# Convolution taps and softplus read PSUM, a product moves to GpSimd, norms and head masks to ScalarE

## The chip, the cores and the metric

The kernel runs on one core of a Trainium2 chip. The metric is the device time of one execution in microseconds. Names of engines in the rows: PE is TensorE, DVE VectorE, ACT ScalarE, POOL GpSimd, SP SyncE.

## The reference, cut to what matters

Sixteen sequences of 512 tokens by 256 features, all fp32, go through two blocks with residuals. "Block 0" is a quadratic-kernel attention with 16 heads of 16 features and an int8-weight gated FFN; "block 1" is a two-way Mamba and an FFN whose operands are quantised to FP4.

```python
x = x + attn(layernorm(x)); x = x + ffn_int8(layernorm(x))
x = x + bimamba(layernorm(x)); x = x + ffn_fp4(layernorm(x))
# attn, per head: A = (q k^T)**2 * causal; o = A v / (A.sum(-1) + eps)
# bimamba(x): xn = norm(x) * g + b; x + mamba(xn, f) + flip(mamba(flip(xn), b))
# mamba: u = silu(causal_conv4(u) + convb)             512 channels
#        dt = softplus(dtr @ Wdt.T + bdt); A = -exp(Alog)
#        h_t = exp(dt_t * A) * h_{t-1} + (dt_t * u_t) * B_t    16 states
#        y_t = sum_n h_t[n] * C_t[n];  y = (y + u * D) * silu(z) @ Wout.T
# q(x) = fp4(x / s) * s per block of 16, s = max|x| / 6
```

## The kernel before

**Timetable.** The recurrence sets the frame. One sequence has 2 directions x 16 states x 4 channel tiles = 128 *slots*; in slot j VectorE runs one `tensor_tensor_scan` over 512 tokens (`scan`, L1216). Around it, with fixed offsets in slots, GpSimd makes the input product B x (dt u) three slots ahead (`inflow`, L714), ScalarE the decay exp(dt A) into PSUM two slots ahead (`decay`, L923), TensorE turns a state back to tokens with four transposes four slots later (`turn_state`, L1501, two PSUM banks HT[0] and HT[1]), VectorE adds half of the turned states weighted by C (`add_state`, L1227), and ScalarE with GpSimd the other half (`weigh_last` L931, `add_last` L725). A state (4 slots) has three buffers, the decay three PSUM banks. So the engines can be a few slots apart and no more.

**The rest of the model** is laid beside this by hand: `PLAN` says for each engine and slot which pieces it issues after the slot's own work (`row(piece, direction, ahead, PE=[...], ACT=[...], ...)`, L285 to L371; `side` issues them). Each engine issues in this order, so a piece that waits holds everything behind it on its engine, the next scan too. While the Mamba of sequence b runs, the attention and int8 FFN of b+1, the FP4 FFN of b-1 and the first steps of b+2 run in its gaps. Direction r=1 is the first half of the slots, its convolution at slots 14 to 25 and its softplus at 35 to 46; r=0 of the next sequence has them at 91 to 98 and 105 to 111.

**PSUM.** Three banks (`SB`) serve all side pieces. `bank_of` gives each product the bank longest unused in the order of `PLAN`; `take_bank` (L411) makes TensorE wait until the reader of the bank's last user is done (`LEAVES` names the signal). From slot 14 to 51 the bank `SUMS` belongs to the attention's weighted sums, so that two are left (`HELD`).

**The pieces that the change touches.** `norm` (L1029) for the five layer norms: three small operations for 1/sqrt, then four `tensor_scalar` of 128x256 (L1042). `attn_q`: a projection of q for 8 heads (L1295) is multiplied by four 0/scale columns to isolate heads, two on ScalarE (L780), two on VectorE (L1062); the four results lie in `qm`, read by the scores (`score`, L1310) of 24 score steps; the second half's projection at PE slot 28 follows the last score of the first. `project` (L844): ScalarE copies the product into the padded `upad` (L856) and writes tap 3 with the bias (L857); `convolve` (L1156): VectorE adds the other three taps from `upad`. `softplus` (L873): Abs and Relu from PSUM (L879, L880), Exp (L882) and Ln (L886) in SBUF; `softplus_rest` (L1169, L1171) makes a rounding correction, `softplus_sum` (L697, L700) adds both on GpSimd, `step_size` (L1176) forms dt u on VectorE. `attn_divide` (L1068) waits for the turned sums.

## Time and profile before

| | |
|---|---|
| time, median of 3 runs | 6962.02 us (6948.84 to 6964.09) |
| the profiled execution: time, span | 6966.85 us, 6965.1 us |
| mean granted TensorE clock | 0.803 |
| one sequence, from a scan to the same scan of the next | 416.2 us |

The page gives busy times of engines over the span; each instruction group by line with what ended the idle time before it; the chain of waits that ended last. Since the sequences repeat, a table of busy times over the stretches of one sequence shows what each part of the timetable is bound by. The sequence that starts at 3231.79 us is used: slot 8 is at 3249.54, 24 at 3293.27, 40 at 3352.37, 48 at 3377.62, 64 at 3423.56, 80 at 3472.24, 96 at 3524.82, 112 at 3591.08 and its end at 3647.94.

### The profile page before, as it was taken

The numbers are of one execution on the slowest core, as the hardware profiler recorded it, in microseconds if no ns is written. First come the engines' busy times: TensorE is split into PE (matmuls) and PEld (weight loads), VectorE is DVE, ScalarE is ACT, GpSimd is POOL, SyncE is SP. The second block draws the span as 40 slices with busy tenths as digits, with TensorE's granted clock in tenths as the row PEclk, the third lists the DMA queues.
The fourth block names the chain that finished last, engine by engine and source line by source line (L and its number), as shares of the span: only waits on it lengthen the run. The fifth ranks groups of instructions, "written<-read, shape, count | busy, mean of one in ns | idle before, by whom it ended". The sixth has DMA issues, their size and how long they took to land.

```text
span 6965.1 us, 83507 instructions
## 1 busy us (share of the span) xinstructions
PE 5063.0 (73%) x21853; PEld 3220.5 (46%) x21900; DVE 5281.2 (76%) x6580; ACT 4022.4 (58%) x6424; POOL 4972.3 (71%) x3786
## 2 busy tenths in 40 slices
PE   3776777868777686877868777676877768777665
PEld 2344444544444444544444444444544444444444
DVE  3277788787878778788787878878787787878884
ACT  1365665656656565655656656565665656656563
POOL 0177877777777777777778777777777777777894
PEclk6688888878878788887878878788887878888777
DMA  3011111111111111111111111111111111111110
GB/s 107 25 36 40 43 48 49 34 50 43 39 50 50 44 34 44 45 48 50 45 43 39 38 51 48 45 33 44 47 48 48 47 43 38 40 48 45 37 46 25
DMA packets 152821, 309.07 MB, mean 44 GB/s; under 512 B 20870, under 2 KB 58310, under 8 KB 149926
## 3 DMA queue, kind: packets, MB, share of 16 engines
q1 hardware_dynamic: 152278, 302.80, 13.5%
q8 instruction: 222, 3.64, 0.2%
q14 instruction: 321, 2.63, 0.1%
HBM read 285.90 MB, written 16.84 MB: 43 GB/s over the span
## 4 chain that ended last, share of the span: by engine, by line
PE 32%; issue 21%; DVE 17%; POOL 17%; ACT 10%; DMA 0%; DVEq 0%; POOLq 0%; SPq 0%; ACTq 0%
POOL arena_m L714 7%; PE psum L1310 7%; PE psum L1501 6%; DVE arena_m L1216 5%; POOL arena_m L725 5%; PE psum L1354 3%; DVE arena_m L1227 2%; PE psum L1273 2%; PE psum L1443 2%; PE psum L1481 2%; ACT hc L931 2%; ACT L759 2%; PE psum L1417 2%; PE psum L1389 1%; DVE arena_m L1156 1%
## 5 line engine op out<-in xcount | busy, mean ns | idle before, releaser
L714 POOL TENSOR_TENSOR arena_m<-bS,arena_m 128x512 f32<-128x512 f32 x2048 | 2703.6, 1334 | 394.7 <-PE psum L1501 358.7
L1216 DVE TENSOR_TENSOR_SCAN arena_m<-psum,arena_m 128x512 f32<-128x512 f32 x2048 | 2452.0, 1209 | 138.4 <-POOL arena_m L714 58.0
L923 ACT ACTIVATE psum<-arena_m,Aneg 128x512 f32<-128x512 f32 x2048 | 1414.8, 694 | 1387.1 <-DVE arena_m L1216 1355.7
L1501 PE MATMUL psum<-ident,arena_m 128*128 128x128 f32 x8192 | 1491.2, 317 | 858.2 <-DVE arena_m L1227 643.5
L725 POOL TENSOR_TENSOR arena_m<-arena_m,hc 128x512 f32<-128x512 f32 x1024 | 1362.9, 1331 | 821.1 <-ACT hc L931 766.5
L1501 PEld LDWEIGHTS psum<-ident,arena_m 128*128 128x128 f32 x8192 | 1121.2, 162 | 1563.4 <-issue 601.3
L1227 DVE SCALAR_TENSOR_TENSOR arena_m<-psum,Ct,arena_m 128x512 f32<-128x512 f32 x1024 | 746.4, 729 | 286.2 <-PE psum L1501 261.3
L1310 PE MATMUL psum<-arena_a 64*128 64x512 f32 (+3 forms) x2048 | 789.0, 517 | 98.7 <-ACT arena_a L790 49.3
L931 ACT ACTIVATE hc<-psum,Ct 128x512 f32<-128x512 f32 x1024 | 695.0, 679 | 229.4 <-PE psum L1501 172.8
L790 ACT ACTIVATE arena_a<-psum 128x384 f32<-128x384 f32 (+1 forms) x768 | 399.6, 526 | 356.1 <-PE psum L1310 352.4
L1310 PEld LDWEIGHTS psum<-arena_a 64*128 64x128 f32 x2048 | 382.9, 214 | 353.4 <-issue 217.1
L1156 DVE SCALAR_TENSOR_TENSOR arena_m<-arena_m,convw 128x512 f32<-128x512 f32 x384 | 421.3, 1098 | 103.4 <-ACT arena_m L857 98.5
L1389 PE MATMUL psum<-wB,arena_a 128*128 128x352 f32 x1024 | 426.4, 549 | 6.3 <-ACT arena_m L880 4.8
L671 POOL TENSOR_TENSOR arena_a<-arena_a 128x704 f32<-128x704 f32 (+1 forms) x80 | 152.3, 1904 | 375.8 <-DVE arena_a L982 375.8
L1354 PE MATMUL psum<-arena_a,wA 128*128 128x512 bf16 x1105 | 323.8, 441 | 104.5 <-ACT arena_m L896 55.9
L662 POOL TENSOR_SCALAR_AFFINE_SELECT arena_a<-arena_a 128x512 f32<-128x512 f32 (+1 forms) x192 | 186.3, 970 | 259.4 <-ACT arena_a L790 259.3
L1408 PE MATMUL psum<-ident,arena_a 128*128 128x128 f32 (+1 forms) x384 | 89.3, 398 | 311.6 <-POOL arena_a L677 311.6
L1176 DVE TENSOR_TENSOR arena_m<-arena_m 128x512 f32<-128x512 f32 x128 | 218.7, 1709 | 110.9 <-POOL arena_m L700 110.9
L1265 PE MATMUL psum<-ident,arena_a 128*128 128x128 f32 x640 | 131.6, 373 | 226.3 <-DVE arena_a L1042 201.4
L1426 PE MATMUL psum<-xnT,wU 128*128 128x512 f32 x512 | 264.0, 642 | 4.7 <-ACT arena_m L857 2.0
L1434 PE MATMUL psum<-xnT,wZ 128*128 128x512 f32 x512 | 264.9, 644 | 0.0
L1389 PEld LDWEIGHTS psum<-wB,arena_a 128*128 128x128 f32 x1024 | 213.8, 231 | 90.4 <-issue 41.8
(151 smaller groups left out, 7524.0 us busy)
## 6 DMA issues: line engine op xcount, KB each, us to landing
bS<-brow SPq DMA_DIRECT2D x512, 256.0 KB, 3.2
wB<-kept_B SPq DMA_DIRECT2D x16, 1408.0 KB, 6.8
wU<-kept_U SPq DMA_DIRECT2D x32, 512.0 KB, 4.3
wZ<-kept_Z SPq DMA_DIRECT2D x32, 512.0 KB, 4.5
wO<-kept_O SPq DMA_DIRECT2D x32, 512.0 KB, 4.8
wA<-kept_A SPq DMA_DIRECT2D x16, 768.0 KB, 7.0
...
```

Of the source, the lines that this page charges most:

```text
L714: pool.tensor_tensor(hb[s % HBS][:, m, :], bS[:, s % 2, :], du[r][:, m, :], ALU.mult).then_inc(m_dbu.sem, 1)
L725: pool.tensor_tensor(yT[:, 2 + i, :], yT[:, 2 + i, :], hc[:, i, :], ALU.add).then_inc(m_yl.sem, 1)
L790: act.activation(asq[:, gu % 2, j, 0:n], bank("a_score", None, w)[:, 0:n], ACT.Square).then_inc(a_sq.sem, 1)
L923: act.activation(EB[j % EBS], dt[r][:, m, :], ACT.Exp, scale=Aneg[:, r, m, n:n + 1]).then_inc(m_dA.sem, 1)
L931: act.activation(hc[:, i, :], HT[1], ACT.Copy, scale=Ct[:, r, 2 + i, n:n + 1]).then_inc(m_hc.sem, 1)
L1156: dve.scalar_tensor_tensor(u[:, m, :], upad[:, m % 2, tap:tap + T], convw[:, r, m, tap:tap + 1], u[:, m, :], ALU.mult, ALU.add).then_inc(m ...
L1216: dve.tensor_tensor_scan(v, EB[j % EBS], v, 0.0, ALU.mult, ALU.add).then_inc(m_scan.sem, 1)
L1227: dve.scalar_tensor_tensor(yT[:, i, :], HT[0], Ct[:, r, i, n:n + 1], yT[:, i, :], ALU.mult, ALU.add).then_inc(m_y.sem, 1)
L1310: ins = pe.matmul(bank("a_score", None, w)[:, c:c + n], kT[rows, ht, i * P:(i + 1) * P], qm[rows, j, i * P:T], start=True, stop=True)
L1354: ins = pe.matmul(bank(piece, None, m), w[:, k, m * P:(m + 1) * P], xparts[:, c, k, :], start=(k == 0 and c == 0), stop=(k == KD - 1 and c ...
L1389: ins = pe.matmul(bank(piece, None, w)[:, 0:FIH], xTq[:, k, i * P:(i + 1) * P], w_[:, k, c * FIH:(c + 1) * FIH], start=(k == 0), stop=(k = ...
L1501: ins = pe.transpose(HT[pos % 2][:, m * P:(m + 1) * P], hb[s % HBS][:, m, i * P:(i + 1) * P], ident[:, :])
```

## The change

1. **Convolution.** `upad`, its copy and its zero pads go. ScalarE writes tap 3 to `u`; the three others are read by VectorE from PSUM, shifted by writing to `u[late:]`, all three in one slot. The bank is free only when the third tap is done.
2. **Softplus.** `ex` goes: Abs and Exp stay in the PSUM bank, and the correction reads it there, now after Ln. The bank is free at the end of the correction instead of after Relu.
3. **dt u** moves to GpSimd, right behind the two additions of the same tile.
4. **Norms.** VectorE keeps the small operations, one more of them (`shift` = -mean x rstd); ScalarE does the 128x256 ones, a slot later.
5. **Head masks** are all on ScalarE. The second half's q is projected right behind the first's (slots 125 and 126 of the sequence before) and copied to `qraw`; each of its masks is written as soon as the last score that reads that slice of `qm` is done.
6. **Timetable.** Consumers come later: the chain from `a_onturn` to the Mamba's `m_turn` moves by 1 to 7 slots, r=0's convolution from 91 to 99, its softplus from 105 to 112. `z_in` of r=1 moves from 80 to 77. The FP4 FFN starts 2 slots earlier (`q_gate` at 88, not 90), and its turn comes 10 slots behind a token tile's first product, not 9. r=1's ScalarE and VectorE steps come one slot earlier. `xTq` has its own place, and a bank that is open between two pieces is not given out.

```diff
-            row("p_conv", r, ahead, DVE=[j0 + c + k for c in late for k in (2, 2, 3)])
+            row("p_conv", r, ahead, DVE=[j0 + c + 2 - r for c in late for k in range(PAD)])
...
-            "p_in": (1, lambda r, n: [(m_up, 2 * (NM * r + n + 1))]), "p_x": (2, lambda r, n: [(m_xd, r + 1)]),
-            "p_c": (1, lambda r, n: [(m_ct, r + 1)]), "p_dt": (1, lambda r, n: [(m_rl, NM * r + n + 1)]),
+            "p_in": (1, lambda r, n: [(m_conv, PAD * (NM * r + n + 1))]), "p_x": (2, lambda r, n: [(m_xd, r + 1)]),
+            "p_c": (1, lambda r, n: [(m_ct, r + 1)]), "p_dt": (1, lambda r, n: [(m_c2, NM * r + n + 1)]),
...
+                pool.wait_ge(*m_sum.by(b, 2 * q + 2))
+                pool.tensor_tensor(du[r][:, m, :], dt[r][:, m, :], u[:, m, :], ALU.mult).then_inc(m_du.sem, 1)
...
+            def norm(b, n, src, dst):
+                act.wait_ge(*ln_scale[n].by(b, 4))
+                for i in range(NT):
+                    act.activation(dst[:, i, :], src[:, i, :], ACT.Identity, scale=rstd[:, n, i:i + 1],
+                                   bias=shift[:, n, i:i + 1]).then_inc(ln_out[n].sem, 1)
...
             def attn_q(b, _, h):
                 act.wait_ge(*a_q_ps.by(b, h + 1))
-                for j in range(2):
+                if h:
+                    act.copy(qraw[:, :], bank("a_q", None, h)).then_inc(a_qr.sem, 1)
+                    return
+                for j in range(G):
                     act.activation(qm[:, j, :], bank("a_q", None, h), ACT.Copy, scale=qmask[:, j:j + 1]).then_inc(a_qa.sem, 1)
+            def attn_qmask(b, _, j):
+                act.wait_ge(*a_s_ps.by(b, NG * NU * G // 2 - G + j + 1))
+                act.wait_ge(*a_qr.by(b, 1))
+                act.activation(qm[:, j, :], qraw[:, :], ACT.Copy, scale=qmask[:, j:j + 1]).then_inc(a_qa.sem, 1)
...
-                act.copy(upad[:, m % 2, PAD:PAD + T], src).then_inc(m_up.sem, 1)
...
-                act.activation(ex[:, c, :], src, ACT.Abs, bias=bdt[:, r, m:m + 1]).then_inc(m_ab.sem, 1)
                 act.activation(dt[r][:, m, :], src, ACT.Relu, bias=bdt[:, r, m:m + 1]).then_inc(m_rl.sem, 1)
+                act.activation(src, src, ACT.Abs, bias=bdt[:, r, m:m + 1]).then_inc(m_ab.sem, 1)
                 act.wait_ge(*m_ab.by(b, q + 1))
-                act.activation(ex[:, c, :], ex[:, c, :], ACT.Exp, scale=-1.0).then_inc(m_ex.sem, 1)
+                act.activation(src, src, ACT.Exp, scale=-1.0).then_inc(m_ex.sem, 1)
...
-                dve.scalar_tensor_tensor(u[:, m, :], upad[:, m % 2, tap:tap + T], convw[:, r, m, tap:tap + 1], u[:, m, :],
+                dve.scalar_tensor_tensor(u[:, m, late:T], src[:, 0:T - late], convw[:, r, m, tap:tap + 1], u[:, m, late:T],
                                          ALU.mult, ALU.add).then_inc(m_conv.sem, 1)
...
-                dve.wait_ge(*m_ex.by(b, q + 1))
+                dve.wait_ge(*m_ln.by(b, q + 1))
```

Three places of the instruction order follow, each before and then after. In them lines of the change are numbered anew: L939, L947 are the decay and `weigh_last`, L811 the squared score, L801 the mask from `qraw`, L1210 the scan, L1221 `add_state`, L719 `inflow`, L730 `add_last`, L674 to L680 the tail of the FP4 rounding (L671 to L677 before).

ScalarE where the attention's second half of heads begins, slots 26 to 29, before:

```order
L790 ACTIVATE arena_a<-psum 128x384
L923 ACTIVATE psum<-arena_m,Aneg 128x512
L790 ACTIVATE arena_a<-psum 128x384 x2
L923 ACTIVATE psum<-arena_m,Aneg 128x512
L931 ACTIVATE hc<-psum,Ct 128x512
L790 ACTIVATE arena_a<-psum 128x384
L923 ACTIVATE psum<-arena_m,Aneg 128x512
L780 ACTIVATE arena_a<-psum,qmask 128x512 x2
L790 ACTIVATE arena_a<-psum 128x512
```

The same place of the change:

```order
L811 ACTIVATE arena_a<-psum 128x384
L939 ACTIVATE psum<-arena_m,Aneg 128x512
L801 ACTIVATE arena_a<-qraw,qmask 128x512 x2
L811 ACTIVATE arena_a<-psum 128x384 x2
L939 ACTIVATE psum<-arena_m,Aneg 128x512
L947 ACTIVATE hc<-psum,Ct 128x512
L801 ACTIVATE arena_a<-qraw,qmask 128x512 x2
L811 ACTIVATE arena_a<-psum 128x384
L939 ACTIVATE psum<-arena_m,Aneg 128x512
L811 ACTIVATE arena_a<-psum 128x512
```

Two masks behind the last score of the first half have become four, two of them ahead of the last three squared scores, and none needs a product of TensorE in between.

VectorE at the first convolution of r=1, slots 13 to 16, before (L1216 and L1210 are the scan):

```order
L1227 SCALAR_TENSOR_TENSOR arena_m<-psum,Ct,arena_m 128x512
L1216 SCALAR_TENSOR_TENSOR arena_m<-psum,arena_m 128x512 x2
L1227 SCALAR_TENSOR_TENSOR arena_m<-psum,Ct,arena_m 128x512
L1156 SCALAR_TENSOR_TENSOR arena_m<-arena_m,convw 128x512 x2
L1216 SCALAR_TENSOR_TENSOR arena_m<-psum,arena_m 128x512
L1156 SCALAR_TENSOR_TENSOR arena_m<-arena_m,convw 128x512
```

The same place of the change:

```order
L1221 SCALAR_TENSOR_TENSOR arena_m<-psum,Ct,arena_m 128x512
L1210 SCALAR_TENSOR_TENSOR arena_m<-psum,arena_m 128x512
L1160 SCALAR_TENSOR_TENSOR arena_m<-psum,convw,arena_m 128x509
L1160 SCALAR_TENSOR_TENSOR arena_m<-psum,convw,arena_m 128x510
L1160 SCALAR_TENSOR_TENSOR arena_m<-psum,convw,arena_m 128x511
L1210 SCALAR_TENSOR_TENSOR arena_m<-psum,arena_m 128x512
```

The taps of a tile stand together, a slot earlier, and read PSUM.

GpSimd at the softplus of r=0, the second of its four tiles, slot 108 before:

```order
L714 TENSOR_TENSOR arena_m<-bS,arena_m 128x512
L697 TENSOR_TENSOR arena_m<-arena_m 128x512
L700 TENSOR_TENSOR arena_m<-arena_m 128x512
L714 TENSOR_TENSOR arena_m<-bS,arena_m 128x512
L725 TENSOR_TENSOR arena_m<-arena_m,hc 128x512
L671 TENSOR_TENSOR arena_a<-arena_a 128x704
```

The same tile in the change, slot 115 (the first tile's three operations stand behind L674, in slot 114):

```order
L674 TENSOR_TENSOR arena_a<-arena_a 128x704
L700 TENSOR_TENSOR arena_m<-arena_m 128x512
L703 TENSOR_TENSOR arena_m<-arena_m 128x512
L705 TENSOR_TENSOR arena_m<-arena_m 128x512
L719 TENSOR_TENSOR arena_m<-bS,arena_m 128x512
L730 TENSOR_TENSOR arena_m<-arena_m,hc 128x512
L677 TENSOR_TENSOR arena_a<-arena_a 128x704
L680 TENSOR_TENSOR arena_a<-arena_a 128x704
L700 TENSOR_TENSOR arena_m<-arena_m 128x512
L703 TENSOR_TENSOR arena_m<-arena_m 128x512
L705 TENSOR_TENSOR arena_m<-arena_m 128x512
L719 TENSOR_TENSOR arena_m<-bS,arena_m 128x512
```

L705 is dt u. The four tiles now fall in four slots in a row, 114 to 117, together with the last FP4 rounding.

## Rows read from the trace of the kernel before

**Rows 1.** The page: span, and part 1, busy time of each engine.
```profile
span 6965.1 us, 83507 instructions
...
PE 5063.0 (73%) x21853; PEld 3220.5 (46%) x21900; DVE 5281.2 (76%) x6580; ACT 4022.4 (58%) x6424; POOL 4972.3 (71%) x3786
```

**Rows 2.** Part 4 of the page: the chain that ended last, by engine.
```profile
PE 32%; issue 21%; DVE 17%; POOL 17%; ACT 10%; DMA 0%; DVEq 0%; POOLq 0%; SPq 0%; ACTq 0%
```

**Rows 3.** Busy time by stretch, one sequence: stretch, length, engines, PEclk, DMA share, GB/s.
```profile
3249.54:3293.27 43.73, 43.52 (x201) 26.06 (x200) 37.54 (x46) 29.65 (x53) 40.51 (x32) 0.96 0.16 50
3293.27:3352.37 59.10, 52.62 (x204) 26.67 (x202) 35.62 (x40) 37.95 (x66) 35.98 (x31) 0.80 0.07 23
3352.37:3377.62 25.25, 23.14 (x107) 11.89 (x107) 20.85 (x23) 19.14 (x35) 25.02 (x20) 0.86 0.07 23
3377.62:3423.56 45.94, 25.29 (x123) 17.78 (x123) 38.38 (x56) 23.84 (x36) 34.04 (x27) 0.74 0.17 58
3423.56:3472.24 48.68, 42.36 (x230) 31.61 (x231) 37.24 (x46) 29.60 (x41) 36.38 (x28) 0.93 0.10 32
3472.24:3524.82 52.58, 40.09 (x156) 24.65 (x154) 44.53 (x71) 34.37 (x53) 36.43 (x27) 0.87 0.21 73
3524.82:3591.08 66.26, 41.62 (x159) 26.92 (x160) 54.32 (x62) 46.21 (x70) 51.18 (x36) 0.79 0.04 13
3591.08:3647.94 56.86, 31.36 (x134) 22.75 (x133) 43.86 (x56) 20.69 (x36) 39.01 (x31) 0.71 0.23 71
```

**Rows 4.** The same view, 20 us inside the second stretch.
```profile
3309.00:3329.00 20.00, 18.68 (x44) 7.84 (x44) 7.51 (x8) 8.26 (x15) 11.14 (x10) 0.61 0.00 1
```

**Rows 5.** Groups by shape, VectorE: what is removed or changed; busy us, mean ns, idle.
```profile
L1156 DVE SCALAR_TENSOR_TENSOR arena_m<-arena_m,convw 128x512 f32<-128x512 f32 x384 | 421.3, 1098 | 103.4 <-ACT arena_m L857 98.5
...
L1171 DVE TENSOR_TENSOR arena_m<-arena_m 128x512 f32<-128x512 f32 x128 | 178.0, 1390 | 4.4
...
L1176 DVE TENSOR_TENSOR arena_m<-arena_m 128x512 f32<-128x512 f32 x128 | 218.7, 1709 | 110.9 <-POOL arena_m L700 110.9
...
L1169 DVE TENSOR_SCALAR arena_m<-arena_m 128x512 f32<-128x512 f32 x128 | 86.8, 678 | 3.6 <-ACT arena_m L882 3.6
...
L1042 DVE TENSOR_SCALAR arena_a<-xA,mv,ve 128x256 f32<-128x256 f32 x192 | 118.1, 676 | 1.2
...
L1042 DVE TENSOR_SCALAR arena_a<-arena_a,mv,ve 128x256 f32<-128x256 f32 x64 | 43.7, 742 | 0.6
...
L1042 DVE TENSOR_SCALAR arena_a<-xF,mv,ve 128x256 f32<-128x256 f32 x64 | 22.9, 421 | 0.0
...
L1062 DVE TENSOR_SCALAR arena_a<-psum,qmask 128x512 f32<-128x512 f32 x64 | 45.1, 746 | 108.8 <-ACT arena_a L780 108.8
```

**Rows 6.** Timeline around 3530 and 3589 us: start us, us, engine, line, operation.
```profile
3527.30 0.75 DVE L1156 SCALAR_TENSOR_TENSOR arena_m<-arena_m,convw 128x512 f32<-128x512 f32 x1
...
3530.18 2.82 DVE L1156 SCALAR_TENSOR_TENSOR arena_m<-arena_m,convw 128x512 f32<-128x512 f32 x2
...
3530.34 2.11 POOL L671 TENSOR_TENSOR arena_a<-arena_a 128x704 f32<-128x704 f32 x1 [7.29 <-DVE arena_a L982]
...
3589.35 1.26 POOL L714 TENSOR_TENSOR arena_m<-bS,arena_m 128x512 f32<-128x512 f32 x1
```

**Rows 7.** Groups by shape: the nearest rows to what is added.
```profile
L1227 DVE SCALAR_TENSOR_TENSOR arena_m<-psum,Ct,arena_m 128x512 f32<-128x512 f32 x1024 | 746.4, 729 | 286.2 <-PE psum L1501 261.3 <-ACT arena_m L896 24.7
...
L714 POOL TENSOR_TENSOR arena_m<-bS,arena_m 128x512 f32<-128x512 f32 x2048 | 2703.6, 1334 | 394.7 <-PE psum L1501 358.7 <-DMA bS<-brow 33.9
...
L857 ACT ACTIVATE arena_m<-psum,convb,convw 128x512 f32<-128x512 f32 x128 | 101.0, 789 | 0.0
...
L827 ACT COPY arena_a<-psum 128x352 f32<-128x352 f32 x128 | 57.7, 450 | 31.5 <-PE psum L1389 31.4
...
L1034 DVE SCALAR_TENSOR_TENSOR lnv<-mv 128x4 f32<-128x4 f32 x80 | 50.2, 628 | 3.1 <-ACT mv L767 3.1
```

**Rows 8.** Groups by shape: the wait for the turned sums.
```profile
L1068 DVE RECIPROCAL rz<-psum 128x16 f32<-128x16 f32 x64 | 16.3, 255 | 178.3 <-PE psum L1333 178.3
```

More of the change, by code:

```diff
@@ L324, in block_kernel @@
[L324 to L338 removed]
+            row("q_up", None, -1, first=2 * i, PE=[j + 3, j + 4], DVE=[j + 4, j + 6])
@@ new lines, in block_kernel @@
+            row("q_hquant", None, -1, first=QHEAD * i, DVE=[j + 6, j + 6, j + 6, j + 7, j + 7, j + 8])
+            row("q_htail", None, -1, first=QTAIL * i, POOL=[j + 8, j + 9, j + 9])
+            row("q_hturn", None, -1, first=2 * i, PE=[j + 10, j + 10], ACT=[j + 11, j + 11])
+            row("q_down", None, -1, first=i, PE=[j + 12], DVE=[j + 13])
+        for j, r, ahead in ((30, 1, 0), (107, 0, 1)):
+            row("p_x", r, ahead, PE=[j, j + 1], ACT=[j + 2])
+            row("p_rows", r, ahead, SP=[j + 3])
+            row("p_c", r, ahead, PE=[j + 4], DVE=[j + 5])
@@ L390, in block_kernel @@
         }
[L391 removed]
+        HELD = range(14, 53)
         jobs_of = [[], [], []]
```

227 lines of the change are left out of this document (99 added, 128 removed).

## The prediction

> **What bounds the kernel now.** I start with the page. Over the span VectorE is busy 76%, TensorE 73%, GpSimd 71% [rows 1]: no engine is full. The chain that ended last is spread over all of them, with TensorE 32%, VectorE and GpSimd 17% each, ScalarE 10% and 21% in which nothing is seen to run [rows 2]. So the kernel is bound by different engines in turn and by the hand-overs between them, and VectorE's sum alone decides nothing. The next view is one sequence cut into stretches [rows 3]; slots 0 to 8, the 17.8 us ahead of its first row, are not touched. The reader should compare each stretch with its busiest engine. Slots 8 to 24 (first row) take 43.7 us and TensorE is busy 43.5: full. Slots 24 to 40 take 59.1 with TensorE at 52.6, at a granted clock of 0.80. Slots 40 to 48 are GpSimd's (25.0 of 25.3). Slots 48 to 64 take 45.9, VectorE 38.4. Slots 64 to 80 lie nearest to TensorE (42.4 of 48.7), slots 80 to 96 to VectorE (44.5 of 52.6). Slots 96 to 128 take 123.1, VectorE 98.2 and GpSimd 90.2, and the end holds some us of the loop's own turn.
>
> **VectorE's sum.** Removed: the 128x256 norms, 118.1 + 43.7 + 22.9 = 184.7 us, the masks, 45.1, and dt u, 218.7 [rows 5]. The 384 taps take 1098 ns now [rows 5]; the same operation with one operand in PSUM takes 729 [rows 7], so they save 384 x 0.369 = 142. The 128 subtractions at 1390 ns [rows 5] become the like, 128 x 0.66 = 85 saved. The addition beside them goes from 678 to about 729, +7, and the 80 `shift` operations cost some 628 ns each, +50 [rows 7]. Together 618 us, 39 per sequence.
>
> Why a tap costs 1098 is seen in the timeline: one alone takes 0.75 us, two beside a GpSimd addition take 1.41 each, and GpSimd's L671 takes 2.11 [rows 6]. The two engines hold each other up when VectorE reads two operands from SBUF. GpSimd's product takes 1.26 alone [rows 6] against a mean of 1.334 [rows 7], so GpSimd would get back up to 2048 x 0.07 = 150 us if all such meetings ended.
>
> The Trainium skill (VectorE: DVE Perf Modes, "Why PSUM operands drop a tier") speaks against the other half of the softplus edit: one-source fp32 operations run twice as fast only between SBUF tensors. The trace shows L1169 between SBUF tensors at a mean of 678, no better than a PSUM operation here; if its mean were half of 729, the edit would lose 128 x 0.36 = 47 us of VectorE instead of 7.
>
> **ScalarE.** Added are 320 norms of 256 columns. Their price lies between a plain copy of 352 columns, 450 ns, and a scaled and biased one of 512, 789 ns [rows 7]; for 256 columns I take 570, nearer the lower end: 182 us. The 80 more masks and q copies stand against the 128 copies to `upad` that go, about zero. ScalarE comes to 4200 us, 60%. That is hidden where ScalarE waits; between slots 26 and 29 it gets four masks for two, which the waits that go there cover.
>
> **GpSimd.** 128 x 1.27 = 163 us more, 10 per sequence: that is a term on the path where GpSimd is full.
>
> **Where the time comes and goes, per sequence.**
> - Slots 8 to 24: **+4**. A convolution's bank was free after two ScalarE operations; now it waits for ScalarE's 0.8 and three taps of 0.73, about 3.3 us with the hand-overs. TensorE has 1.5 to 2.4 us of other work before it needs that bank for the second score of the next slot. It stalls at slots 17, 20 and 23, 0.9 to 1.8 us each, 4.4 together, less some for the shorter VectorE part; behind it wait the transposes of the state. Bounds: -1 (the taps are done in time) and +8 (each waits a scan more).
> - Slots 24 to 40: **-7**. The masks of the second half no longer stand in a row after a new projection. TensorE ran at half its clock from 3309 to 3329 us: 18.7 us busy at a granted 0.61, for the most part at the lower of its two levels, 1.2 of 2.4 GHz [rows 4]; at full clock that is 18.7 x 0.61 = 11.4, or 7.3 less, and its idle 1.3 us goes. VectorE's wait for the turned sums, 178 us in all or 11 per sequence, two of its four places here [rows 8], ends in part, since its piece now comes a slot later. Against it: ScalarE's softplus of 4 operations and the correction now hold a bank about 4.7 us at slots 35 and 38, with 2.5 us of cover, so +4.4 if nothing hides it; I count half. Bounds: -12 and +2.
> - Slots 40 to 48: **+4**. Three dt u on the full engine, 3 x 1.27. The two bank stalls there, 2.2 us each, lie beside GpSimd's work. Bounds +3 and +5.
> - Slots 48 to 64: **-7**. Eight norm operations leave VectorE (8 x 0.58 = 4.6), and the projection behind the attention gets a slot more between its steps, so that VectorE does not stand before it. Bounds: -10 and -2.
> - Slots 64 to 80: **+2**. The int8 FFN starts 5 slots later with the same TensorE work, after a longer idle time in which the clock falls (0.74 in the stretch ahead, [rows 3]). Bounds -1 and +4.
> - Slots 80 to 96: **-6**. Eight norm operations, 4 x 0.676 + 4 x 0.742 = 5.7 us, and eight taps of r=0, 8.8, leave VectorE [rows 5]; FP4 and int8 pieces that move in and four small operations fill part of it, and ScalarE's norms now stand between the steps of a chain. I count less than half. Bounds: -9 and -1.
> - Slots 96 to 128: **-4**. VectorE loses four dt u, 6.8, four norms, 2.7, four longer subtractions, 2.6, two masks, 1.5, and has twelve taps at 0.73 for four at 1.10, +4.4: 9.2 less. GpSimd gets the four softplus tiles in slots 114 to 117: 4 x 3 x 1.27 = 15.2, three FP4 operations of at most 2.1 each [rows 6], 6, and its own 4 x (1.27 + 0.64) = 7.6, in all 29 us for four slots; the product for the scan three slots on stands behind them, and VectorE has fewer pieces than that in these slots. What VectorE wins before that is largely waited for here. Bounds: -14 and +6.
>
> Sum: 4 - 7 + 4 - 7 + 2 - 6 - 4 = **-14 us per sequence**, 224 for sixteen (the first and last are partly alone, which I leave out). The profiled execution took 6966.85 us, 5 more than the median of the runs. 6966.85 - 224 = 6743; against the median 6738. I predict **6740 us**.
>
> **Rivals.**
> 1. *Held banks decide, slower.* The place is TensorE behind p_in and p_dt with two banks. If VectorE is a scan and an addition late at the third tap, each of the first three stalls is 3 us instead of 1.4, and slots 8 to 24, 43.5 us of TensorE at 0.96, run at the 0.80 of the next stretch: 43.5 x 0.96/0.80 - 43.5 = 8.7. With that and no clock won back in slots 24 to 40 (-1 for -7) the sum is 3 x 3 + 8.7 - 1, and -11 for the other five terms: +6, or 7060 us. For: TensorE is full there. Against: VectorE has fewer and shorter operations just there, and ScalarE's step comes a slot earlier. The sign turns when the seven stalls are 2 us longer each than I assume. The Trainium skill (TensorE: Matmul & The Clock Gate, Part 1) says that throttled is the default and activity releases it; that would make this rival costlier than its stalls. Chance 0.13.
> 2. *All of VectorE's time comes back.* If every stretch gave VectorE's 39 us, 16 x 39 = 618, the time would be 6350. For: VectorE is the busiest engine, and GpSimd gains too. Against: TensorE and GpSimd would then need 311 us each within 378, closer than in any long stretch now but the first. The Trainium skill (SBUF — State Buffer, "Who interferes with whom") says that only VectorE operations with two SBUF inputs or in a 2-port mode meet GpSimd, so that with one operand in PSUM both gain. Between 6500 and this: chance 0.12.
> 3. *Nothing but waiting moves.* The load leaves VectorE, but each stretch is set by hand-overs (21% of the chain, [rows 2]) and the gains of slots 24 to 40 fail, -1 for -7, and 48 to 64, -2 for -7: so 3 us less per sequence in place of 14: 6920, with the places nearest to no change among its outcomes. Chance 0.08.
> 4. *GpSimd's cluster costs the gain at the end*, +6 for -4, so 4 us less per sequence in all: 6900. For: the count above. Against: GpSimd's bound stretch before, 104 to 111, held eight such additions too. Chance 0.05.
>
> **How the numbers follow.** The forecast case, 6540 to 6860, has 0.62. The distances of the bounds from the seven terms, taken together as independent, give about 16 us per sequence upward and 13 downward: 6990 and 6530. I stretch the lower end to 6480 for the nearer part of the second rival; the range is **6480 to 6990**. Within 0.2% is about what a measurement of this kernel can tell from no change. Faster by more: 0.62 + 0.12 + most of rivals 3 and 4 = 0.83. The same: 0.04, from rival 3. Slower: 0.13.
>
> **What would show it.** In the profile after: taps at 0.70 to 0.75 us with or without GpSimd beside them; VectorE's busy time near 4660 us; norms on ScalarE near 0.57; TensorE waiting for VectorE's third tap in score products at slots 17, 20, 23, 1 to 2 us each; slots 24 to 40 shorter with a clock above 0.9; GpSimd full at slots 114 to 118 with scans waiting for its product. I am wrong if TensorE's waits behind held banks pass 3 us each, if slots 24 to 40 keep their 59 us, or if 96 to 128 grow.

## The result and the profile after

The changed kernel takes **6918.5 us** (median of 11 runs, 6890.6 to 6958.3) against 6962.0 (11 runs); the ratio is 0.9942, 95% interval 0.9921 to 0.9962. It is faster by 0.6%, not by the 3.2% of the forecast: the direction is right, the time lies in the range, the size is missed by 179 us. The kernel before took 6962 us beside the change and 6948 to 6953 beside the experiments below, so differences across them are good to about 10 us. One run of e4 (9407 us) and one of e12 (13041 us) lie far above the others of their kernel and enter no ratio.

The page of the kernel after, span and part 1 [rows 1], and part 4, the chain [rows 2]:

```profile
span 6935.8 us, 82733 instructions
...
PE 5245.0 (76%) x21900; PEld 3287.9 (47%) x21900; DVE 4746.4 (68%) x6116; ACT 4128.6 (60%) x6696; POOL 4905.2 (71%) x3914
...
PE 41%; issue 19%; POOL 18%; DVE 10%; ACT 9%; DMA 2%; POOLq 0%; SPq 0%; DVEq 0%; ACTq 0%
```

VectorE lost 535 us of work, and the span 29. TensorE has the same matmuls and is busy 182 us longer (some 20 of them because 47 matmuls are missing from the trace before); its share of the chain rose from 32 to 41%. The mean granted clock is 0.803, as before. So the load went away, and the end is now set more by TensorE and what it stands for.

The groups by shape, kernel after (busy us, mean ns | idle before and what ended it) [rows 5, 7, 8]:

```profile
L719 POOL TENSOR_TENSOR arena_m<-bS,arena_m 128x512 f32<-128x512 f32 x2048 | 2599.3, 1285 | 183.2 <-PE psum L1493 155.3 <-DMA bS<-brow 26.1 <-issue 1.2
...
L778 ACT ACTIVATE arena_a<-xA,shift,ve 128x256 f32<-128x256 f32 x192 | 99.7, 594 | 61.4 <-DVE shift L1055 61.4
...
L872 ACT ACTIVATE arena_m<-psum,convb,convw 128x512 f32<-128x512 f32 x128 | 99.2, 775 | 204.4 <-PE psum L1418 204.1
...
L1160 DVE SCALAR_TENSOR_TENSOR arena_m<-psum,convw,arena_m 128x509 f32<-128x509 f32 x128 | 95.2, 744 | 190.6 <-ACT arena_m L872 190.6
...
L1176 DVE TENSOR_TENSOR arena_m<-psum,arena_m 128x512 f32<-128x512 f32 x128 | 88.5, 691 | 4.4
...
L1174 DVE TENSOR_SCALAR arena_m<-psum 128x512 f32<-128x512 f32 x128 | 87.9, 687 | 309.9 <-ACT arena_m L899 268.0 <-POOL arena_m L703 41.9
```

The durations are those of the prediction: taps 744 to 750 ns for 729, norms 594 for 570, the subtraction 691. The idle column is not. The first tap (L1160) stood 191 us for ScalarE's tap 3 (98.5 in [rows 5]) and the correction (L1174) 268 us for ScalarE's Ln, where its predecessor L1169 waited 3.6 [rows 5]. ScalarE itself stood 204 us for the projection.

The waits of the whole span, kernel after (us in total, times, longest). L1303 is the squared score's product, L1176 and L1160 VectorE's last readings of a softplus's and a convolution's bank, L892 the softplus's first operation and L899 its Ln, L872 ScalarE's tap 3:

```profile
DVE arena_m L1174 <- ACT arena_m L899: 268.0, 67, 8.0
...
ACT arena_m L892 <- PE psum L1448: 213.4, 97, 4.0
...
ACT arena_m L872 <- PE psum L1418: 204.1, 87, 5.4
...
DVE arena_m L1160 <- ACT arena_m L872: 190.6, 78, 9.4
...
PE psum L1303 <- DVE arena_m L1176: 127.1, 60, 2.9
...
PE psum L1381 <- DVE arena_m L1160: 81.3, 28, 3.6
...
PE psum L1303 <- DVE arena_m L1160: 70.1, 45, 2.0
...
PE psum L1448 <- DVE arena_m L1176: 44.8, 16, 3.2
```

The two of L1303 are the held banks that the prediction named: 105 stalls, 2.1 and 1.6 us each. The other two stalls of TensorE behind VectorE it did not count: the FP4 FFN's products (L1381) stand behind the convolution of r=0, and the softplus's own products (L1448) behind the correction, 126 us together. The four waits of VectorE and ScalarE were not in it either. They are one chain: TensorE's product and ScalarE's reading are in one slot, VectorE's reading is in the next, and each engine stands until the one ahead of it is done, with the next scan behind it.

The relief of VectorE did reach TensorE: its transposes of the state waited 643.5 us for VectorE's `add_state` before and wait 285.3 us after. The span is shorter by 29 us all the same.

Busy time by stretch of the sequence that starts at 3207.27 us (columns as in [rows 3]; slots 8 to 24, 24 to 40, 40 to 48, 48 to 64, then 80 to 96):

```profile
3227.48:3278.88 51.40, 46.03 (x195) 26.82 (x194) 35.71 (x49) 28.27 (x50) 37.05 (x32) 0.90 0.14 44
3278.88:3338.09 59.21, 52.67 (x190) 26.38 (x190) 31.57 (x38) 36.30 (x62) 35.84 (x31) 0.73 0.07 21
3338.09:3370.00 31.91, 27.11 (x95) 14.42 (x95) 15.34 (x20) 18.99 (x35) 22.84 (x20) 0.66 0.08 17
3370.00:3410.96 40.96, 26.84 (x139) 18.09 (x138) 31.11 (x42) 26.94 (x43) 37.02 (x31) 0.79 0.18 61
...
3461.25:3508.84 47.59, 38.43 (x168) 27.81 (x167) 38.17 (x60) 34.86 (x56) 34.09 (x27) 0.82 0.25 81
```

Slots 8 to 24 took 43.73 us and take 51.40, at a clock of 0.90 for 0.96; slots 40 to 48 took 25.25 and take 31.91, at 0.66 for 0.86, and GpSimd, full there before, idles 9 us. From slot 48 on the gains are there.

Single sequences differ by some us, so the same cut is averaged over ten sequences (the fourth to the thirteenth), from the starts of the scans in the trace, in us; e-numbers are the experiments below.

```
slots      0-8   8-24  24-40  40-48  48-64  64-80  80-96  96-128   sum
before    17.8   43.8   59.1   25.2   46.0   48.7   52.6   123.2  416.4
after     19.6   52.6   56.8   31.2   40.6   49.5   47.3   114.7  412.2
e1        18.8   51.5   50.4   32.8   41.6   48.3   46.6   115.1  405.1
e2        19.6   52.4   53.9   25.1   40.7   49.1   47.1   115.3  403.2
e3        19.3   52.1   49.3   23.6   41.6   49.3   46.6   114.2  395.9
e4        19.8   56.1   69.5   41.8   41.5   48.7   47.4   114.4  439.2
e5        19.2   50.3   63.3   32.5   41.5   49.4   47.3   114.9  418.4
e6        17.8   51.4   49.4   26.8   39.0   49.0   46.4   113.8  393.6
e7        20.2   52.3   49.3   23.6   45.3   48.8   52.4   114.3  406.2
e8        17.8   51.4   52.1   27.8   41.1   49.8   47.8   117.5  405.1
e9        17.4   47.1   56.6   29.2   40.2   49.5   47.3   118.1  405.4
e10       19.1   44.3   52.1   25.2   36.2   49.3   47.1   116.2  389.5
e11       17.7   51.5   69.9   33.1   48.2   48.7   52.6   120.9  442.7
e12       17.7   50.4   70.8   32.2   50.3   48.9   52.6   123.1  446.1
```

Ten sequences win 4.2 us each, 42 in all; the first scan starts 21 us earlier; the other six sequences and the end give 34 back, 22 of them in the fifteenth, which took 391 us before and 413 after (why is not shown). Together that is the 29 us between the spans.

Slots 24 to 40 are not alike in the ten sequences of the changed kernel. The shortest and the longest:

```profile
4109.42:4159.31 49.89, 43.17 (x194) 22.51 (x194) 31.25 (x38) 36.73 (x63) 35.81 (x31) 0.90 0.08 25
...
4924.11:4983.33 59.22, 52.67 (x190) 26.36 (x190) 31.58 (x39) 36.30 (x62) 35.83 (x31) 0.73 0.07 22
```

TensorE's busy time times its clock is nearly the same, 38.9 and 38.4 us, and so is its idle time, 6.7 and 6.6 us: the work is equal, and the 9 us between the two are the granted clock. Two of the ten have the short form (49.9 and 51.2 us, at 0.90 and 0.85), eight take 57.6 to 59.2 us at 0.73 to 0.79; the sequence shown above is one of the longest. On average the clock there is 0.79, for 0.78 before, and in e3 it is 0.90 in all ten. What tips a sequence one way or the other was not found.

### The profile page after: what moved, and what is told of

The parts are those of the page before. It is cut to its first block, busy times and chain, and to the rows that moved or that the text cites. A ratio compares the mean times of both kernels' runs of the same rounds, so it can differ in the third digit from the quotient of the medians.

```text
span 6935.8 us, 82733 instructions
## 1 busy us (share of the span) xinstructions
PE 5245.0 (76%) x21900; PEld 3287.9 (47%) x21900; DVE 4746.4 (68%) x6116; ACT 4128.6 (60%) x6696; POOL 4905.2 (71%) x3914
## 4 chain that ended last, share of the span: by engine, by line
PE 41%; issue 19%; POOL 18%; DVE 10%; ACT 9%; DMA 2%; POOLq 0%; SPq 0%; DVEq 0%; ACTq 0%
PE psum L1303 9%; POOL arena_m L719 9%; PE psum L1493 8%; POOL arena_m L730 5%; PE psum L1347 3%; PE psum L1473 3%; PE psum L1426 3%; PE psum L1363 2%; DVE arena_m L1160 2%; PE psum L1418 2%; PE psum L1318 2%; DVE arena_m L1210 2%; POOL arena_a L677 2%; PE psum L1448 1%; PE psum L1435 1%
## 5 line engine op out<-in xcount | busy, mean ns | idle before, releaser
L719 POOL TENSOR_TENSOR arena_m<-bS,arena_m 128x512 f32<-128x512 f32 x2048 | 2599.3, 1285 | 183.2 <-PE psum L1493 155.3
L1210 DVE TENSOR_TENSOR_SCAN arena_m<-psum,arena_m 128x512 f32<-128x512 f32 x2048 | 2448.4, 1210 | 345.4 <-ACT psum L939 170.2
L1493 PE MATMUL psum<-ident,arena_m 128*128 128x128 f32 x8192 | 1524.6, 323 | 661.3 <-DVE arena_m L1221 285.3
L730 POOL TENSOR_TENSOR arena_m<-arena_m,hc 128x512 f32<-128x512 f32 x1024 | 1307.3, 1277 | 1009.6 <-ACT hc L947 829.4
L1493 PEld LDWEIGHTS psum<-ident,arena_m 128*128 128x128 f32 x8192 | 1166.0, 167 | 1413.7 <-issue 738.4
L939 ACT ACTIVATE psum<-arena_m,Aneg 128x512 f32<-128x512 f32 x2048 | 1397.6, 689 | 389.9 <-DVE arena_m L1210 375.3
L1221 DVE SCALAR_TENSOR_TENSOR arena_m<-psum,Ct,arena_m 128x512 f32<-128x512 f32 x1024 | 750.5, 733 | 512.4 <-PE psum L1493 511.0
L1303 PE MATMUL psum<-arena_a 64*128 64x512 f32 (+3 forms) x2048 | 895.3, 568 | 227.9 <-DVE arena_m L1176 127.1
L947 ACT ACTIVATE hc<-psum,Ct 128x512 f32<-128x512 f32 x1024 | 693.9, 678 | 362.9 <-PE psum L1493 278.7
L811 ACT ACTIVATE arena_a<-psum 128x384 f32<-128x384 f32 (+1 forms) x768 | 400.8, 524 | 547.2 <-PE psum L1303 546.6
L1303 PEld LDWEIGHTS psum<-arena_a 64*128 64x128 f32 x2048 | 411.8, 230 | 589.7 <-issue 288.1
L1381 PE MATMUL psum<-wB,arena_m 128*128 128x352 f32 x1024 | 451.0, 575 | 97.3 <-DVE arena_m L1160 81.3
L1160 DVE SCALAR_TENSOR_TENSOR arena_m<-psum,convw,arena_m 128x509 f32<-128x509 f32 (+2 forms) x384 | 286.9, 747 | 199.6 <-ACT arena_m L872 190.6
L674 POOL TENSOR_TENSOR arena_a<-arena_a 128x704 f32<-128x704 f32 (+1 forms) x80 | 144.6, 1807 | 366.9 <-DVE arena_a L998 366.9
L1347 PE MATMUL psum<-arena_a,wA 128*128 128x512 bf16 x1152 | 307.8, 411 | 102.1 <-ACT arena_m L909 38.9
L1381 PEld LDWEIGHTS psum<-wB,arena_m 128*128 128x128 f32 x1024 | 218.7, 236 | 202.3 <-DVE arena_m L1160 74.6
L1174 DVE TENSOR_SCALAR arena_m<-psum 128x512 f32<-128x512 f32 x128 | 87.9, 687 | 309.9 <-ACT arena_m L899 268.0
L1426 PE MATMUL psum<-xnT,wZ 128*128 128x512 f32 x512 | 255.1, 623 | 1.5 <-DVE xM L1193 1.5
L1473 PE MATMUL psum<-wO,arena_m 128*128 128x256 f32 x1024 | 245.8, 384 | 0.9 <-DVE arena_m L1184 0.9
```

The lines of the kernel that those rows point to most:

```text
L719: pool.tensor_tensor(hb[s % HBS][:, m, :], bS[:, s % 2, :], du[r][:, m, :], ALU.mult).then_inc(m_dbu.sem, 1)
L730: pool.tensor_tensor(yT[:, 2 + i, :], yT[:, 2 + i, :], hc[:, i, :], ALU.add).then_inc(m_yl.sem, 1)
L939: act.activation(EB[j % EBS], dt[r][:, m, :], ACT.Exp, scale=Aneg[:, r, m, n:n + 1]).then_inc(m_dA.sem, 1)
L947: act.activation(hc[:, i, :], HT[1], ACT.Copy, scale=Ct[:, r, 2 + i, n:n + 1]).then_inc(m_hc.sem, 1)
L1210: dve.tensor_tensor_scan(v, EB[j % EBS], v, 0.0, ALU.mult, ALU.add).then_inc(m_scan.sem, 1)
L1221: dve.scalar_tensor_tensor(yT[:, i, :], HT[0], Ct[:, r, i, n:n + 1], yT[:, i, :], ALU.mult, ALU.add).then_inc(m_y.sem, 1)
```

## The experiments

**e1, e2, e3: banks given back early.** r=1 alone goes back to copies in SBUF (there is room for one direction only): in e1 its taps read a padded copy, in e2 Abs and Exp of its softplus go to `qraw` and the correction reads it there, after Exp; e3 is both. ScalarE then frees the bank by itself, at the same slots as in the change. r=0 still reads PSUM. (In the diff, `...` stands for lines left out, here and below.)

```diff
-"p_in": (1, lambda r, n: [(m_conv, PAD * (NM * r + n + 1))])
+"p_in": (1, lambda r, n: [(m_up, NM + n + 1), (m_cp, n + 1)] if r else [(m_conv, PAD * (n + 1))])
...
-"p_dt": (1, lambda r, n: [(m_c2, NM * r + n + 1)])
+"p_dt": (1, lambda r, n: [(m_rl, NM + n + 1), (m_ab, NM + n + 1)] if r else [(m_c2, n + 1)])
...
+act.copy(upad[:, m % 2, PAD:PAD + T], src).then_inc(m_cp.sem, 1)
...
+e = qraw[:, :] if r else src
```

> The changed kernel, but direction r=1 (slots 13 to 25, where two banks are left) takes its taps from a padded SBUF copy again; the bank is free after ScalarE's two operations. Held banks decide: the bank waits behind p_in in slots 17, 20, 23 go (45 waits, 70 us in all, behind the taps in the score products) and VectorE no longer gates them; slots 8 to 24 go from 52.8 us back to about 45, the kernel to about 6800 us. Rival, VectorE's early pieces decide (its taps stand a slot earlier and wait for ScalarE, so the scan behind waits): the taps still stand in the same slots, slots 8 to 24 stay above 50 us, 6900 us or more.

> The changed kernel, but the softplus of r=1 keeps Abs and Exp in SBUF (the q copy's place, free then), and frees its bank after Relu and Abs. Held banks decide: TensorE's 60 waits for the correction in the score products, 127 us in all, go; slots 32 to 48 lose about 8 us per sequence, the kernel comes to about 6800 us. Rival, the order of ScalarE's four operations and VectorE's place decide: VectorE still waits for ScalarE's Exp, which ends 0.7 us earlier only, and it meets GpSimd again; less than 3 us per sequence, 6880 us or more.

> Both of the above. Held banks decide: the first half of the slots comes back to what the kernel before needs there or less, 14 to 16 us per sequence, 6680 to 6700 us. Early VectorE pieces decide: 6860 us or more. If both matter the two single runs add up to less than this one.

Measured: e1 6810.2 us (ratio 0.9799, 0.9775 to 0.9823), e2 6766.1 (0.9731, 0.9705 to 0.9757), e3 6664.0 (0.9625, 0.9563 to 0.9687). Against the changed kernel that is 108, 152 and 254 us less. The two are nearly additive, and in this order of the rows the reading of PSUM by VectorE costs 254 us for r=1, though its taps and subtractions got shorter by it. The times are near those expected of held banks. But slots 8 to 24 stay at 51.5 to 52.4: the held bank is not what made them long, as I had expected of e1. The time came back from slot 24 on; in e1 slots 24 to 40 lose 6.4 us, and the granted clock there is 0.86 for 0.79. What is left in slots 8 to 24 is seen in the waits of e3 in that stretch, 3084.51 to 3136.66 us (L884 copies the projection, L885 writes tap 3, L1182 is a tap):

```profile
ACT arena_m L884 <- PE psum L1449: 10.3, 4, 3.6
DVE arena_m L1182 <- ACT arena_m L885: 10.2, 4, 3.7
```

Four tiles, 2.5 us each, on two engines one behind the other. In the same stretch of the kernel before they are 1.3 and 0.2 us, in the changed kernel 10.0 and 11.0.

**e4, e5: r=1's consumers a slot later.** The change puts ScalarE's and VectorE's pieces of r=1 one slot earlier than before (`- r`). e4 takes that back in the changed kernel, e5 in e3. (In e5, and in e10 below, ScalarE also waits for its own Ln of the tile before, since `qraw` is written again.)

```diff
-ACT=[j0 + c + 1 - r for c in late] ... DVE=[j0 + c + 2 - r for c in late for k in range(PAD)]
+ACT=[j0 + c + 1 for c in late] ... DVE=[j0 + c + 2 for c in late for k in range(PAD)]
```

> The changed kernel with r=1's ScalarE and VectorE steps of convolution and softplus one slot later, as in r=0; PSUM still read. Held banks decide: the bank is held longer, TensorE waits more, 6950 to 7050 us. Early VectorE pieces decide: VectorE's waits for Ln (268 us) and for tap 3 (191 us) shrink, the scans are earlier, 6850 us or less.

> The run with both r=1 edits in SBUF, and r=1's ScalarE and VectorE steps a slot later, as in the kernel before. Without held banks a later reader costs TensorE nothing. Theory that the early place blocks the scans (VectorE's 11 us of waits for tap 3 in slots 8 to 24 of one sequence, none before): slots 8 to 24 go from 52.1 to about 44 us, the kernel to about 6540 us. Rival, that these slots are full of TensorE's work at a lower clock and the place is indifferent: 6640 to 6690 us.

Measured: e4 7328.7 us (1.0550, 1.0522 to 1.0579), e5 6995.1 (1.0059, 1.0039 to 1.0079). Every theory failed here. For held banks e4 is too slow by 280 us; for the early place both have the wrong sign, and e5 has no bank held by VectorE. The waits of e5 say who holds it instead (whole span; L1335 is the score's product, L912 and L885 ScalarE's last readings of the two banks, L816 ScalarE's square of the scores):

```profile
ACT arena_a L816 <- PE psum L1335: 859.6, 436, 5.9
...
PE psum L1335 <- ACT qraw L912: 120.6, 60, 2.5
...
PE psum L1335 <- ACT arena_m L885: 91.1, 45, 2.4
```

TensorE waits for ScalarE and ScalarE for TensorE. The kernel before has the same pieces at the same slots and only 352 us of the first wait. What differs is the order within a slot: `side` issues the pieces of a slot in the order of the table's rows, and the change also moved the rows of `p_in`, `p_conv`, `p_silu`, `p_dt` and `p_du` behind the attention's. I had overlooked that in the diff.

**e6, e7, e8: single edits taken back, each in e3.** dt u on VectorE again (e6); the 128x256 norms on VectorE again, their ScalarE slot now VectorE's (e7); the masks again as before, two on each engine, the second projection at slot 28 (e8).

```diff
-pool.tensor_tensor(du[r][:, m, :], dt[r][:, m, :], u[:, m, :], ALU.mult).then_inc(m_du.sem, 1)
+dve.tensor_tensor(du[r][:, m, :], dt[r][:, m, :], u[:, m, :], ALU.mult).then_inc(m_du.sem, 1)
...
-row("f_norm", None, 1, DVE=[61], ACT=[62])
+row("f_norm", None, 1, DVE=[61, 62])
...
-row("a_q", None, 2, PE=[125, 126], ACT=[126, 127])
-row("a_qmask", None, 1, ACT=[27, 27, 28, 28])
+row("a_q", None, 2, PE=[125], ACT=[126], DVE=[126])
+row("a_q", None, 1, first=1, PE=[28], ACT=[29], DVE=[29])
```

> The run with both r=1 edits in SBUF (6664 us), with dt u on VectorE again, two slots later than the additions, as before. If moving it gained what left VectorE (8 products of 1.7 us, 14 us per sequence): 6850 us. If GpSimd is the bound where it went (1.27 us each, slots 40 to 48 and 112 to 118): 6640 us or less. I expect between, 6720 us: a cost of 3 to 4 us per sequence, from the meetings of the two engines more than from the sum.

> The run with both r=1 edits in SBUF, with the twenty 128x256 norm operations of a sequence on VectorE again, in the slot in which ScalarE does them. Theory that VectorE bounds slots 48 to 64 and 80 to 96 (12 operations there, 0.6 us each): 5 to 8 us per sequence more, 6770 us. Rival, that the slots given between the steps did it and the engine is indifferent: 6650 to 6690 us.

> The run with both r=1 edits in SBUF, with the second half's q projected at slot 28 again and its masks split over ScalarE and VectorE. The prediction's term: slots 24 to 40 go from 49.3 us up by 6 to 8 and TensorE's clock falls there, 6770 us. Rival, that the banks did it: within 1 us per sequence, 6680 us.

Measured: e6 6642.8 us (0.9554, 0.9535 to 0.9573), e7 6823.1 (0.9804, 0.9773 to 0.9834), e8 6816.0 (0.9797, 0.9775 to 0.9819). So on e3 the norms on ScalarE are worth 159 us, more than the 106 that I said; the time is in slots 48 to 64 and 80 to 96, 3.7 and 5.8 us per sequence, where the prediction has it. The masks are worth 152, again more than the 106 that I said, but slots 24 to 40 have only 2.8 us per sequence of them, not the 6 to 8 that I had expected; 4.2 are in slots 40 to 48 and 5.0 from slot 64 on. I had expected dt u back on VectorE to cost 56 us. It costs nothing: e6 is the faster by 21 us, which is not clear of noise, since the intervals overlap.

**e9, e10: a slot later, and the rows back ahead of the attention's.** e9 is e4 with the block of rows moved; e10 is e6 with both edits. (With the early place the block can't stand ahead: at slot 34 ScalarE would wait for a product that waits for a score's bank, whose reading stands behind on ScalarE. I read that in the plan; this form was not run.)

```diff
+        for j0, j, r, ahead in ((13, 30, 1, 0), (97, 107, 0, 1)):
+            ...
         row("z_in", 0, 0, PE=[46, 47, 48, 50], ACT=[47, 48, 49, 51])
...
-        for j0, j, r, ahead in ((13, 30, 1, 0), (97, 107, 0, 1)):
-            ...
```

> The changed kernel with r=1's ScalarE and VectorE pieces one slot after the product (as the kernel before has them) and, unlike e4, with the rows of p_in, p_conv, p_dt and p_du back ahead of the attention's in the table, so that within a slot the convolution's and the softplus's pieces come before the squared scores. PSUM is still read by VectorE. Theory O (order within the slot): in e4 ScalarE's piece that reads the bank stands behind a squared score whose product comes at the end of the slot, so TensorE waits for ScalarE and ScalarE for TensorE; with the order of before that lock goes: slots 24 to 48 at 85 to 95 us instead of e4's 111, the time 6900 to 7050, at least 250 below e4's 7329. Theory H (held banks alone): the bank still waits for VectorE a slot later, and the time stays at 7250 or more. A time below the changed kernel's 6919 would mean that the earlier place of r=1 itself costs even with banks held.

> The same two edits (one slot later, and ahead of the attention's rows) on the fastest kernel so far, e6, in which r=1's taps and softplus read SBUF copies and dt u is VectorE's. Theory O: VectorE no longer stands for ScalarE, nor ScalarE for TensorE's projection (10 us each in slots 8 to 24 of e3), and the bank is free after two ScalarE operations at the head of the slot: slots 8 to 24 at 44 to 46 us for 51, the whole at 6500 to 6600. Theory H, or any in which the later place itself costs as in e5: 6900 or more.

Measured: e9 6816.0 us (0.9788, 0.9760 to 0.9815), e10 6550.9 (0.9410, 0.9385 to 0.9434). The order takes 513 us from e4. e9 is 102 below the changed kernel with the same banks held, and 84 below the 6900 that I had given as its least. In e10, as expected, slots 8 to 24 are at 44.3 us; slots 24 to 48 are no shorter than in e6 (77.3 us for 76.2). The busy time of e10 there and in the two stretches behind, one sequence:

```profile
3045.91:3090.25 44.34, 43.00 (x199) 25.59 (x199) 38.42 (x46) 29.10 (x52) 39.17 (x32) 0.97 0.14 49
3090.25:3141.40 51.15, 47.17 (x202) 24.81 (x200) 35.55 (x42) 39.59 (x69) 36.22 (x31) 0.83 0.08 27
3141.40:3166.64 25.24, 22.78 (x107) 12.30 (x107) 20.80 (x22) 19.50 (x35) 25.01 (x20) 0.86 0.07 22
```

TensorE is full again, at 0.97 of its clock. And two groups of e10's VectorE, r=1's taps from SBUF and dt u:

```profile
L1181 DVE SCALAR_TENSOR_TENSOR arena_m<-arena_m,convw 128x512 f32<-128x512 f32 x192 | 251.1, 1308 | 7.2 <-ACT arena_m L883 2.3
...
L1205 DVE TENSOR_TENSOR arena_m<-arena_m 128x512 f32<-128x512 f32 x128 | 189.5, 1481 | 93.7 <-POOL arena_m L707 93.7
```

The fastest kernel has the slowest taps with a mean of 1308 ns. They lie beside GpSimd again: its instructions cover 75% of their time in the trace, and 32% in e3. They wait 7 us in all, while e3's of 944 ns waited 161. VectorE is busy 5026.8 us in e10, 280 more than after the change, and the kernel is 368 us faster.

**e11, e12: the order alone, in the kernel before.** e11 moves the five rows behind the attention's in the kernel before, all slots unchanged. e12 does it on ScalarE only:

```diff
+for parts in PLAN["ACT"]:
+    parts.sort(key=lambda part: part[0] in ("p_in", "p_silu", "p_dt", "p_du"))
```

> The kernel before, with one edit: the rows of p_in, p_conv, p_silu, p_dt and p_du stand behind the attention's in the table, as the change has them, at the same slots; so only the order within a slot changes, on every engine. Theory O: this alone costs what e5 shows against before in slots 8 to 24, about 6 us per sequence there, and 5 to 15 in slots 24 to 48, together 10 to 20: 7120 to 7280. Rival: order within a slot is worth nothing, 6950 to 6975.

> The kernel before, with e11's order within a slot on ScalarE alone; TensorE, VectorE and GpSimd issue as before. In e11 TensorE's first squared score of the next slot waits 2 to 3 us for ScalarE's reading of p_in and p_dt (L860, L883), and ScalarE's own square waits for TensorE (54 us in slots 8 to 48 for 20 before). Theory S: this ring between the two engines is the whole cost, and one engine's order makes it: 7300 to 7450. Rival: the order on TensorE (the weighted sums ahead of the projection) or on VectorE and GpSimd carries it: 6950 to 7100 here.

Measured: e11 7392.8 us (1.0629, 1.0612 to 1.0647), e12 7428.3 (1.0687, 1.0663 to 1.0710). Another order of the pieces within a slot on one engine, with no instruction added, costs 475 us. ScalarE's order alone costs as much as that of all engines, and e11 is 113 us above the upper end that I had given. What moves is this (ScalarE's instructions in slot 17, the kernel before, then e12, whose lines are numbered 3 higher):

```
L923 ACTIVATE psum<-arena_m,Aneg 128x512
L856 COPY arena_m<-psum 128x512
L857 ACTIVATE arena_m<-psum,convb,convw 128x512
L790 ACTIVATE arena_a<-psum 128x384

L926 ACTIVATE psum<-arena_m,Aneg 128x512
L793 ACTIVATE arena_a<-psum 128x384
L859 COPY arena_m<-psum 128x512
L860 ACTIVATE arena_m<-psum,convb,convw 128x512
```

The timeline of the kernel before at that place (start us, us; L1426 is the projection, L1310 the scores' product):

```profile
3272.03 1.88 PE L1426 MATMUL psum<-xnT,wU 128*128 128x512 f32 x4
...
3273.95 0.59 ACT L856 COPY arena_m<-psum 128x512 f32<-128x512 f32 x1 [0.30 <-PE psum L1426]
...
3275.42 1.57 PE L1310 MATMUL psum<-arena_a 64*128 64x256 f32 x8
...
3276.38 0.49 ACT L790 ACTIVATE arena_a<-psum 128x384 f32<-128x384 f32 x1 [1.16 <-PE psum L1310]
```

And of e12:

```profile
3486.61 1.88 PE L1429 MATMUL psum<-xnT,wU 128*128 128x512 f32 x4
...
3490.01 0.92 PE L1313 MATMUL psum<-arena_a 64*128 64x256 f32 x4
...
3490.96 0.49 ACT L793 ACTIVATE arena_a<-psum 128x384 f32<-128x384 f32 x1 [2.41 <-PE psum L1313]
3491.35 0.58 ACT L859 COPY arena_m<-psum 128x512 f32<-128x512 f32 x1
...
3492.66 0.92 PE L1313 MATMUL psum<-arena_a 64*128 64x256 f32 x4 [1.74 <-ACT arena_m L860]
```

Before, ScalarE empties the projection's bank while TensorE is at other work, and the two scores of the slot follow each other without a gap (x8 in one row). In e12 ScalarE stands 2.41 us for the first score with the projection ready in PSUM, then empties that bank, and the second score waits for it 1.74 us. The waits of e12 over the whole span:

```profile
ACT arena_a L793 <- PE psum L1313: 847.5, 477, 5.9
...
PE psum L1313 <- ACT arena_m L883: 116.2, 60, 2.5
...
PE psum L1313 <- ACT arena_m L860: 89.7, 45, 2.5
```

The kernel before has 352.4 us of the first, 10.9 of the second (15 times) and nothing of the third to speak of. Only 206 us are TensorE's direct stalls behind these two readings; the rest of the 475 is in what follows from them, and the clock falls too: in e12's slots 24 to 40 TensorE is busy 59.08 of 71.11 us at a granted 0.74, where [rows 3] show 52.62 of 59.10 at 0.80.

## Why the prediction was right or wrong

The runs price a path from e10 to the changed kernel. Early place and late rows together, on e6: 6550.9 to 6642.8, 92 us. dt u to GpSimd: 21, not clear of noise. PSUM read by VectorE, r=1: 254. In all 368 lost, against 159 and 152 won by the norms and the masks, and the rest of the gain, some 90 to 100 us, in what these runs did not take apart (r=0's part, the later chain from the attention to the Mamba, the start). So the change holds gains of 400 to 410 us, and gives back 368. The prediction's own terms are 24 us per sequence of gains, 384 in all, and 10 of losses, 160: the gains are near what it counted, and the losses are more than twice as large. The single prices hold on this path; since the parts act on one another, another order of taking them back would share the sum otherwise.

Term by term, in us per sequence, forecast and measured (the table):

- **Slots 8 to 24, +4: measured +8.8, beyond the bound of +8.** This is where the argument failed. The stalls that it counted are there, 70.1 us in 45 times, 1.6 each, 4.7 per sequence with an attention beside it, for 4.4. But e1 removes the held bank and the stretch stays at 51.5. With the later place and the rows ahead, and the bank still held, e9 has 47.1, 3.3 above the kernel before: that is the +4 of the forecast. The other 5.5 us come with the earlier place and the moved rows together, and e10, without the held bank too, has 44.3. The step that failed is that this pair had no price: the sum has no term for the order of the rows, and the first rival counts "ScalarE's step comes a slot earlier" as relief. With the rows behind the attention's the earlier place is in fact the better of the two (the changed kernel against e4, e3 against e5), but the pair costs: ScalarE stands 2.5 us for each of four projections in its own slot, then VectorE as long for ScalarE.
- **Slots 24 to 40, -7: measured -2.3**, and **40 to 48, +4: measured +6.0**, beyond the bound of +5. The gain from the masks is real: e8 without it is longer by 2.8 and 4.2 us in the two. The clock did not rise above 0.9: over the ten sequences it is 0.79 in slots 24 to 40, for 0.78, and 0.67 in 40 to 48, for 0.86. The win of clock for which the term stands came in two sequences of ten. The stalls behind the softplus's bank are 127.1 / 60 = 2.1 us, for 2.2, four per sequence. Two steps failed: that half of the stalls at 35 and 38 is hidden, and that those at 41 and 44 "lie beside GpSimd's work". e2 takes the held bank away and gets 6.1 us back in slots 40 to 48, 2.9 in 24 to 40. And the correction "now after Ln" was given no price: VectorE stood 268 us for it, where it had stood 3.6 for Exp; in e9, with the later place and the same bank, it stands 72. VectorE's wait for the turned sums, which was to end in part, grew from 178 to 217 us (L1075, for L1068 in [rows 8]).
- **Slots 48 to 64, -7: measured -5.4; 64 to 80, +2: +0.8; 80 to 96, -6: -5.3; 96 to 128, -4: -8.5.** All inside their bounds. e7 confirms the cause of two: the norms are worth 3.7 and 5.8 us there. GpSimd's cluster at the end did not cost what the bound allowed: in the sequence shown slots 114 to 118 took 18.5 us with GpSimd busy 16.4, where the prediction counted 29. The waits behind the held banks of r=0, 126 us in all, had no term either and lie inside what these stretches gained.
- **The sum, -14: measured -4.2**, of which +1.8 is in slots 0 to 8, which the prediction took as untouched. The start and end, left out of the sum, add 13 us to the ten sequences' -42.
- **VectorE's busy time, near 4660: 4746.** The taps saved 134 us for 142 and the subtractions 90 for 85, the `shift` operations cost 848 ns and not 628, and other operations grew by some 25 us. The busy times of VectorE's groups, added up, fell by 578 us for the 618; the page's figure fell by 535, since it counts the time that two groups share once.

Of the rivals the first, held banks, names the right place and not the right price: its stalls are 1.6 and 2.1 us, not the 3 from which it would decide, and slots 8 to 24 lost 8.8 us and not its 17.7, most of them by the pair that it took for relief. The second is excluded: 535 us less of VectorE gave 29. In the third, "nothing but waiting moves", the sum (-3, 6920 us) is what was measured, and that is luck: its mechanism is not there, since slots 48 to 64 and 80 to 128 did gain, and slots 8 to 24 lost more than it has. The fourth did not happen.

On two of the rules of the Trainium skill that the prediction names. "Who interferes with whom" (SBUF — State Buffer) says that an operation of VectorE with at most one SBUF input, outside the 2-port modes, does not meet GpSimd. The traces agree: the taps are at 744 to 750 ns in all three shapes for 1098 before, none of the 384 takes more than 751 ns, with GpSimd beside it or not, and GpSimd's product fell from 1334 to 1285 ns, 104 us over 2048 of them. "Why PSUM operands drop a tier" (VectorE: DVE Perf Modes) would make the correction's addition dearer from PSUM. The means do not show it, 687 ns from PSUM for 678 from SBUF before [rows 5], and the prediction took that as an answer. The single times do (least, median and greatest in ns; the kernel before, then after):

```profile
L1169 DVE TENSOR_SCALAR arena_m<-arena_m x128: 393/560/5653, 337.1 to 6653.7; 128x512 f32<-128x512 f32 x128
...
L1174 DVE TENSOR_SCALAR arena_m<-psum x128: 672/691/693, 336.4 to 6619.6; 128x512 f32<-128x512 f32 x128
```

The 16 of L1169 with no GpSimd instruction beside them take 401 to 427 ns, and none from PSUM takes less than 672. So the trace agrees with this rule too: from SBUF the addition is faster alone, and in this kernel it lost that again beside GpSimd.

Left open: which of the two parts of e9's 102 us, the place or the order, carries how much, since the early place with the early order was not run; what of the 475 us of e12, and of the 254 of the PSUM reading, is the fallen clock and what the waits behind the stalls; and what r=0's reading of PSUM costs, since every run from e1 to e10 has it.
